# Router products taken from the gate's turned rows and summed with the rows, and a prologue with weight loads on a second queue

## What is computed

```python
# layer 0: 3x3 local attention on a normed image (group norm, then per-channel norm)
x = x + conv_attention(_gn(x), Wq, bq, Wk, bk, Wv, bv, Wo, bo)
# layer 1, on tokens
t = _to_tokens(x)
n = _ln_t(t)
g = sigmoid(tanh(n @ Wp.T + bp) @ Wg.T)              # the gate, one number per token
t = t + windowed_sum(g * n, 64) / windowed_sum(g, 64)  # running sum over 64 tokens
u = _ln_t(t)
logits = u @ router_w.T                              # 8 experts
# softmax, the two best experts, and for each of them gelu(u @ w1 + b1) @ w2 + b2, weighted
```

## Time and profile before

| what | value |
| --- | --- |
| median of 3 runs | 1447.72 us (1446.48 to 1451.52) |
| the profiled execution's own time | 1442.31 us |
| its span, first to last instruction | 1440.5 us |
| mean granted TensorE clock | 0.941 |
| busy share of the span: PE / PEld / DVE / ACT / POOL | 89% / 78% / 78% / 69% / 52% |
| prologue | 0 to 33.4 us |
| token phase | 33.8 to about 835 us |
| expert phase | about 835 to 1310 us |
| output phase | the rest |

### The profile page before, as it was taken

The page is one execution under the profiler, slowest core; times in us unless marked ns, Lnnn a source line. Parts: engine busy times, 40 slices in busy tenths (PEclk is TensorE's granted clock), DMA queues, the critical chain, the costliest instruction groups (busy, mean ns, idle before and its releaser), DMA issues. The chain is left out here.

```text
span 1440.5 us, 28874 instructions
## 1 busy us (share of the span) xinstructions
PE 1285.4 (89%) x8512; PEld 1130.3 (78%) x8512; DVE 1127.6 (78%) x3903; ACT 987.1 (69%) x2090; POOL 746.9 (52%) x963
## 2 busy tenths in 40 slices
PE   3799999999999999999999589999999999993434
PEld 3688888888888888888887478899999999982334
DVE  5478888888888777878786778899999999983323
ACT  1677777777777777777775468888888888871223
POOL 2115656566656566566655465566566656662000
PEclk9999999999999999999999679999999999996555
DMA  8622535363542122222111189988888888856999
GB/s 273 216 83 80 149 86 148 88 156 89 147 117 91 58 83 64 82 69 86 50 42 57 36 277 326 300 270 270 277 271 270 273 263 275 279 194 273 416 400 350
DMA packets 148216, 264.00 MB, mean 183 GB/s; under 512 B 52576, under 2 KB 74720, under 8 KB 143840
## 3 DMA queue, kind: packets, MB, share of 16 engines
q1 hardware_dynamic: 113440, 173.78, 38.6%
q0 software_dynamic: 25920, 71.60, 14.0%
q10 hardware_dynamic: 8704, 16.78, 3.0%
HBM read 128.39 MB, written 100.68 MB: 159 GB/s over the span
## 5 line engine op out<-in xcount | busy, mean ns | idle before, releaser
L1716 POOL DMA_INDIRECT answers<-yy,dest_i x284 | 276.7, 974 | 176.7 <-DVE yy L1837 99.7
L1558 POOL DMA_INDIRECT sent<-tn,slot_s x256 | 275.5, 1076 | 146.7 <-issue 79.2
L1768 PE MATMUL s_bank<-band,hh 128*128 x568 | 163.2, 287 | 0.6 <-DVE yy L1872 0.6
L1768 PE MATMUL s_bank<-w_s,hh 128*128 x568 | 157.2, 277 | 0.0
L1768 PE MATMUL s_bank<-band,hl 128*128 x568 | 157.0, 276 | 0.0
L1802 ACT ACTIVATE hid<-m_bank,b1s 128x512 f32<-128x512 f32 x142 | 97.7, 688 | 78.3 <-PE m_bank L1751 50.3
L1822 ACT ACTIVATE zz<-xin 128x256 f32<-128x256 f32 x284 | 147.5, 602 | 0.0
L758 PE MATMUL m_bank<-wvo,band 128*128 128x258 f32 x792 | 132.7, 304 | 13.3 <-DVE band L1390 10.9
L1535 POOL TENSOR_TENSOR rs<-ve,halves 128x4 f32<-128x4 f32 x64 | 64.9, 1019 | 153.7 <-DVE ve L1252 153.7
L790 PE MATMUL o_bank<-vv,at 128*128 128x256 f32 x512 | 138.7, 393 | 1.3 <-DVE tt L1300 0.8
L758 PEld LDWEIGHTS m_bank<-wvo,band 128*128 128x128 f32 x792 | 107.1, 192 | 29.4 <-issue 27.7
(11 more groups left out here) (238 smaller groups left out, 3658.9 us busy)
## 6 DMA issues: line engine op xcount, KB each, us to landing
xin<-sent SPq DMA_DIRECT2D x71, 524.0 KB, 4.7
got<-answers SPq DMA_DIRECT2D x32, 1024.0 KB, 9.7
w1hs<-rT SPq DMA_DIRECT2D x71, 256.0 KB
w1ls<-w_s SPq DMA_DIRECT2D x71, 256.0 KB
xs<-in_x SPq DMA_DIRECT2D x32, 512.0 KB, 5.0
raw<-in_x SPq DMA_DIRECT2D x32, 512.0 KB
out_x<-fin ACTq DMA_DIRECT2D x32, 512.0 KB, 10.0
b2s<-in_b SPq DMA_DIRECT2D x71, 128.0 KB
```

The source lines that it names most:

```text
L1558: eng.indirect_dma_start(sent, bass.IndirectOffsetOnAxis(slot_s[:, par, j, k:k + 1], 0), tn[:, par, k, :], None).then_inc(scattered[par], 16)
L1716: eng.indirect_dma_start(answers, bass.IndirectOffsetOnAxis(dest_i[:, at_ % RING, k:k + 1], 0), yy[:, slot, k, :], None).then_inc(rows_out ...
L1768: last = eng.matmul(y_bank[half][:, k * C:(k + 1) * C], hx[:, par, f, ts], rhs, start=(n == 0), stop=(n == 3 * CC - 1))
```

## The change

It has two parts.

1. **Router.** The router's products are computed in stage C from `xn1T`, the turned rows that the gate uses (`router`, now job Crouter, after `gate_product`). The router's weights are centred once in the prologue (each expert's mean over the channels is subtracted), so that the row's mean drops out. DVE's new `routed` writes the 8 products of each token twice: times the row's deviation (`dev1`) into 8 new columns of `tt`, and as they are into 8 new columns of `xn1`. From there they go as 8 columns more through the gating (`wx`), the running sums (266 columns for 258) and `windowed` (264 for 256). In stage D the logits are `tt`'s 8 columns times the inverse deviation of the second norm. `tokens_turned`, `tokens_taken`, the jobs Dtr01 and Dtr23 and the tile `tnT` are gone; `tn` itself is still made, as it is what is sent. The jobs have other banks. On ACT `gates_taken` stands behind `value_taken(it, 2)`.
2. **Prologue.** The 12 weight and bias loads are issued by ACT, the ones needed for the fold first and on a semaphore of their own (`w_fold`); SP begins with `xs`. ACT runs one small activation early. ACT starts to take the first half of the fold when it is done. DVE clears `tail_id`, `blank` and `besti` first of all, takes the statistics of image 0's 8 blocks and their means before the constants, and mixes the chain of the group sums with the statistics of the next 4 blocks. POOL does its two roots before the low parts of the folded weights. After the meeting DVE clears only two columns of `xn1`.

```diff
+        CX = C + E + 2
...
         def prologue_sync(eng):
-            for dst, src in ((wq_s, wqT), (wk_s, wkT), (wv_s, wvT), (wo_s, wo), (wp_s, wpT), (rw_s, rwT)):
-                eng.dma_start(dst[:, :, :], src.rearrange("(c p) n -> p c n", p=P)).then_inc(w_in, 16)
...
         def prologue_gpsimd(eng):
...
+            for n in range(2):
+                group_root(eng, 0, n)
             eng.wait_ge(folded, 2)
...
-            for n in range(2):
-                group_root(eng, 0, n)
             leave(eng, 0)
 
         def prologue_tensor(eng):
-            eng.wait_ge(w_in, 16 * 12)
+            eng.wait_ge(w_fold, 16 * 8)
             eng.wait_ge(dve_const, 1)
...
             eng.wait_ge(pool_const, 23)
+            eng.wait_ge(w_in, 16 * 4)
+            product(s_bank[1], slice(P, P + E), lambda d: ones[:, :], lambda d: rw_s[:, d, :]).then_inc(router_sum, 1)
             for n in range(2):
                 group_product(eng, 0, n, s_bank[1]).then_inc(g_sum, 1)
...
         def prologue_scalar(eng):
-            eng.wait_ge(w_in, 16 * 12)
+            def matrix(dst, src, landed):
+                eng.dma_start(dst[:, :, :], src.rearrange("(c p) n -> p c n", p=P)).then_inc(landed, 16)
+
+            for (dst, src), (bias, given) in (((wq_s, wqT), (bq_s, bq)), ((wk_s, wkT), (bk_s, bk)), ((wv_s, wvT), (bv_s, bv)),
+                                              ((wo_s, wo), (bo_s, bo))):
+                matrix(dst, src, w_fold)
+                eng.dma_start(bias[:, :, :], given.unsqueeze(2)).then_inc(w_fold, 16)
...
         def prologue_vector(eng):
...
+            eng.memset(tail_id[:, :, :, :], 0.0).then_inc(zeroed, 1)
+            eng.memset(blank[:, :, :], 0.0).then_inc(zeroed, 1)
+            eng.memset(besti[:, :, :].rearrange(flat), 0).then_inc(zeroed, 1)
+            eng.wait_ge(w_fold, 16 * 8)
             eng.tensor_copy(bqb[:, :, :], bq_s[:, :, :].broadcast_to([P, CC, P])).then_inc(dve_const, 1)
...
+            for i in range(XR):
+                for c in range(CC):
+                    seen(i, c)
+            eng.wait_ge(x_done[XR - 1], 1)
+            block_means(eng, 0)
...
+            group_spread(eng, 0, s_bank[1])
+            seen(XR, 0)
+            group_variance(eng, 0, s_bank[1])
+            seen(XR, 1)
+            channel_variance(eng, 0)
+            seen(XR + 1, 0)
+            image_scales(eng, 0)
+            seen(XR + 1, 1)
+            for i in range(XR + 2, XR + EARLY):
                 for c in range(CC):
-                    last = eng.bn_stats(stats[:, c, i, :], xs[:, i % XR, c, :])
...
+            eng.wait_ge(router_sum, 1)
+            for c in range(CC):
+                eng.scalar_tensor_tensor(rw_s[:, c, :], s_bank[1][:, P:P + E], -1.0 / C, rw_s[:, c, :], ALU.mult, ALU.add)
...
-        JOBS = ("VV0 AV1 AR0 Epos BX01 AR1 Dtr01 Dtr23 Ctr01 Ctr23 Drouter Cproj AV2 Cgate BX23 AV4 Cwin0 AV3 "
+        JOBS = ("VV0 AV1 AR0 Epos BX01 AR1 Ctr01 Ctr23 Cproj Crouter AV2 Cgate BX23 AV4 Cwin0 AV3 "
                 "Cwin1 Cwin2 Cwin3").split()
...
-                    last = eng.matmul(bank[:, 0:C + 2], band_cur[:, :], wx[:, par, h, k, :], start=(h == 0),
+                    last = eng.matmul(bank[:, 0:CX], band_cur[:, :], wx[:, par, h, k, :], start=(h == 0),
...
             def router(it):
-                moved(it, "Dtr01")
-                moved(it, "Dtr23")
-                bank = begin(it, "Drouter")
+                bank = begin(it, "Crouter")
...
-                        last = eng.matmul(bank[:, k * E:(k + 1) * E], tnT[:, cc, k * P:(k + 1) * P],
+                        last = eng.matmul(bank[:, k * E:(k + 1) * E], xn1T[:, cc, k * P:(k + 1) * P],
...
                     attend(it, 2)
-                if d:
-                    tokens_turned(it, 0)
-                    tokens_turned(it, 2)
                 if c:
                     gated_turned(it, 0)
                     gated_turned(it, 2)
-                if d:
-                    router(it)
                 if b:
                     weigh(it, 1)
                 if c:
                     gate_product(it)
+                    router(it)
...
             def mean_scaled(it):
                 root.wait(eng, it, "Crs1")
+                eng.reciprocal(dev1[:, :], rs[:, 0, :])
...
+            def routed(it):
+                i = bank_of["Crouter"]
+                full[i].wait(eng, it, "Crouter")
...
+                ln1_step.wait(eng, it, "Cms1")
+                products = m_bank[i][:, 0:KT * E].rearrange("p (a b) -> p a b", b=E)
+                eng.tensor_tensor(tt[:, it.block("C") % TT, :, C:C + E], products,
+                                  dev1[:, :].unsqueeze(2).broadcast_to([P, KT, E]), ALU.mult)
+                eng.tensor_copy(xn1[:, :, C:C + E], products).then_inc(taken[i].sem, 1)
+
+            def best_of(it):
+                root.wait(eng, it, "Drs2")
+                step(it, route, "Dlogit", eng.tensor_tensor(logit[:, :, :], tt[:, it.block("D") % TT, :, C:C + E],
+                                                            rs[:, 1, :].unsqueeze(2).broadcast_to([P, KT, E]), ALU.mult))
...
                 if it.off == NB:
                     for x in range(0, 2):
                         lower_parts(eng, x)
+                if c:
+                    routed(it)
                 if b:
                     tokens(it, 1)
```

More of the change, by code:

```diff
@@ L830, in window @@
                         before = wx[:, 1 - par, h, KT - 1, :] if k == 0 else wx[:, par, h, k - 1, :]
-                        last = eng.matmul(bank[:, 0:C + 2], band_prev[:, :], before, start=False, stop=(h == 1))
+                        last = eng.matmul(bank[:, 0:CX], band_prev[:, :], before, start=False, stop=(h == 1))
                 end(last, job)
@@ L861, in router @@
                         last = group_product(eng, image_of(it, 6 - n), n, bank)
-                end(last, "Drouter")
+                end(last, "Crouter")
             def positions(it):
@@ L1011, in gated_rows @@
                 for k in range(KT):
-                    last = eng.activation(xn1[:, k, 0:C], tt[:, it.block("C") % TT, k, :], ACT.Identity,
+                    last = eng.activation(xn1[:, k, 0:C], tt[:, it.block("C") % TT, k, 0:C], ACT.Identity,
                                           bias=mean_rs[:, k:k + 1], scale=rs[:, 0, k:k + 1])
```

92 lines of the change are left out of this document (38 added, 54 removed).

## The result

The changed kernel takes 1456.97 us (median of 20 runs, 1452.47 to 1460.17 but for one of 3737.55), the kernel before 1448.75 beside it: a ratio of 1.0055, with a 95% interval of 1.0043 to 1.0066. It is slower by 8 us, where 13.6 less were forecast; rival C had this side, with a chance of 0.08. The profiled execution took 1457.96 us, its span is 1456.2. Columns before and after are times in us, but for the last row, which counts.

The account below looks back on a forecast made before the run. PE was taken to set the pace, each block's cycle running through ACT's 3.0 us chain to `xn`. Loop -6.3, last iterations -3.8 and prologue -3.5 made -13.6 from 1447.72: 1434.1 us, range 1429 to 1443 (8 in 10: 1425 to 1444.5).

Parts of the forecast that it names:

- rival C: Loop: PE's clock falls in most blocks, 1.7 us each, making the kernel slower, +20 us to 1468; chance 0.08.
- Transposes of `tn`: Token loop on PE: removing eight transposes gains 0, as they lie inside ACT's 3.0 us chain to `xn`.
- Wait for `pT`: Token loop, gate's weight loads: router and `values` together cover the tanh, gaining 0.27 us a block.
- wider sums: Token loop on PE: 16 products get 8 more columns, costing 0.056 us a block.
- Last three iterations: End of the token phase: the router fills waits and a chain goes, -3.8 us, which the expert phase keeps.
- the sum's loop term: Token loop, 30 blocks with all stages: -0.21 us each, -6.3 us in all (-10 to +2).
- the pause: Token loop: a new PE pause of 1 us ahead of the transposes in each block, named as possibly lowering the clock.
- Prologue: Start: `xs` begins earlier, fold weights land at 8.3 us, less clearing; ACT's first instruction at 32.3 for 35.78, -3.5 us.
- The sum: Whole kernel: loop -6.3, last iterations -3.8 and prologue -3.5 make -13.6 us, giving 1434.1 us.

Follow-up runs that it names:

- router_split5: The changed kernel with the router's products in two halves, ahead of and behind the gate's wide product: 1431.08 us, ratio 0.9876 to the kernel before.
- wide_between: The changed kernel with six unused wide products between `values` and the gate per block: 1631.19 us, the kernel before beside it 1607.74 (disturbed series), ratio 1.0145.
- weights_first5: The changed kernel with SyncE issuing the fold's four matrices ahead of `xs`: 1448.56 us, ratio 1.0000 to the kernel before.
- three_mends4: The changed kernel with fold matrices first, router in halves, and GpSimd's low parts waiting for VectorE's image scales: 1421.19 us, ratio 0.9810 to the kernel before.

## Why the prediction was wrong

*Transposes of `tn`, worth 0.* Right. PE's query product of router_split5 starts at 468.96 and the transposes of `xn` at 473.53, 4.57 us later; before it was 427.96 - 423.40 = 4.56. The wait took all of the transposes' time, 0.99 us on PE.

*Wait for `pT`, -0.27, and wider sums, +0.06.* Right in kind, small in size. From transposes to gate router_split5 has 6.28 us with a group product of 0.23 in it, so 6.05 for 6.39; the rest of the block is 0.07 shorter. In the changed kernel a block without a fall changed by -0.2 to -0.5, -0.41 in the middle, not -0.21.

*Last three iterations, -3.8.* Near: the last two intervals of `pT` are 21.56 and 23.50 for 21.82 and 26.03, and 0.35 us more behind them: -3.1. That "the expert phase keeps" it is not shown: behind the last `fell` the changed kernel takes 2.7 us more than the kernel before. But this stretch, which the variants leave alone, lasted 605.1 to 609.5 us in the five undisturbed traces of the changed kernel and its variants, so a loss there isn't shown to be the change's either.

*Rival C.* Here the prediction failed first. It named the place ("router, `values` and gate in a row"), the price (1.7 us, measured 1.65) and the point (slower from 11 more falls; 12 came). It gave 0.08 on the ground that "the longest narrow stretch becomes shorter". That argument is the step that failed: it took one wide group between narrow ones for enough. With 0.8 us of `values` between 1.7 us of router and 0.8 of gate, the clock fell in 14 blocks of 31; with the router's half moved away (router_split5) in none, and six more wide products behind `values` removed the falls behind the row too (wide_between). So the sum's loop term, -6.3 with nothing for falls, was mis-sized by 12 falls, some 20 us. No row of the trace before has such a row of products, so nothing there could price the chance. The other suspect that C named, the pause, was harmless, and here the Trainium skill (TensorE: Matmul & The Clock Gate, HAM oscillation), by which waits of several microseconds bring repeated falls, was no guide either way: the pause of 1 us did nothing, as it would have it, but the falls came without any such wait.

*Prologue, -3.5.* Here it failed second. "I let them land at 8.3 as before, with 10.5 as the late bound": 16.1. The prediction says that the weights share the engines with `xs`, but has no working for 10.5; eight blocks of 512 KB on SP's queue were issued from 0.81 us, beside and ahead of the weights. In place of -3.5, +5.0 was measured. The late weights cost 8.9 (weights_first5; 8.0 where the fold went at the slow pace with early weights too), and the port 2.0, which no term had; without both the start is 6.0 us ahead of the kernel before, at 29.79 in three_mends4, and not 3.5. One sum in this term is off as well: 23.0 and 7.6 make 30.6 and not 30.9. The rule quoted there (the Trainium skill, DMA: Bandwidth & Descriptors, Rules for kernel authors: issuing engines share the same 16 DMA engines) agrees with what the trace shows, and its consequence is larger than I took it to be: it brings not just no gain for the weights but a loss, since what is issued beside them delays them.

*The sum.* Without the falls the change is worth more than was forecast: router_split5 is 16.4 us under the kernel before, with the start, 5 us late, still in it. The falls and the 0.1 us a block give back 25.9 us. That makes 9.5 us lost, against 8.2 measured beside its own kernel before. By the spans, the loop's +7.5 is 12 falls of 1.65, or 19.8, and 1.7 for the double one, less 0.43 in each of 31 blocks, or 13.3: +8.2. That the spans of before and after differ by 15.7 us and the medians by 8.2 stays without a shown cause, since only one execution of the kernel before was profiled, a fast one.

## What to carry to other kernels

When narrow products are moved, write down what TensorE does in the microseconds on either side of their new place, idle time with it, and put wide products between them: here eight narrow products moved by one place were worth 26 us. When loads are moved to a second queue, the first user's bytes must be issued first over all queues together, since the queues share the engines. And where a change puts products in an order that no row of the profile has, the outcome in which the clock takes the gain back deserves a chance of more than 0.08. Which of the two clocks a product ran at is read from its own time, as the clock column can stand at 1.00 beside both.

## What was not expected of the hardware

- Two operations of VectorE on 128x2 took 1.22 and 1.19 us while GpSimd was at TENSOR_TENSORs of 128x512, and 0.16 and 0.17 when these came later. The Trainium skill (SBUF — State Buffer, SBUF: two separate sides) has VectorE and GpSimd share one pair of ports. An operation of VectorE with two inputs in SBUF contends for it with one of GpSimd that reads SBUF, and the one that starts first holds it for the whole instruction. The traces agree, with each of the two starting 0.07 to 0.1 us behind one of GpSimd's and ending with it.
- In the fold, four products of 256 columns took 2.05 us in one execution and 1.11 in another, with the granted clock at 1.00 in both.
- Moving sixteen products of 8 columns changed the number of falls of the clock in 31 blocks from 2 to 14, and splitting them in halves around a wide product to 0.
- The same kernel on the same chip took 1447 us in one series and 1608 in another, and on a second chip 1449 and 1559 to 1565. The traces of its variants in the slower series have waits for TensorE's results in ACT and DVE that no operation in the trace explains.
